# A transformer layer on one core: one gelu for each pair of row tiles, its splits and its second product in later half steps, and the coefficients of one more row tile by GpSimd

## The reference

```python
x = x + attn(layernorm(x))          # x: 8 x 1024 x 512, float32
x = x + ffn(layernorm(x))
# attn: 32 query rows of 16, causal softmax, probs in pairs:
diff = probs[:, :, 0] - lambda_full * probs[:, :, 1]     # 16 heads
attn = einsum('bhqk,bhkd->bhqd', diff, v)                # then RMS norm per head, @ Wo.T
# ffn: weights cut to -1, 0, 1
h = gelu(x @ w1_q.T + b1)           # 512 -> 2048, exact gelu
out = h @ w2_q.T + b2               # 2048 -> 512
```

## Time and profile before

| | |
|---|---|
| runs (three) | 4142.19 us median, 4137.09 to 4144.37 |
| profiled execution, its own time | 4130.02 us |
| its span, first to last instruction | 4128.2 us |
| PE, DVE, ACT, POOL busy | 81%, 80%, 70%, 43% of the span |
| mean granted TensorE clock | 0.938 of full |

### The profile page before, as it was taken

One profiled execution on the slowest core, in us unless ns is written; L12 is line 12 of the kernel. 1 busy time (PEld: TensorE's weight loads), 2 busy tenths in 40 slices (PEclk: granted clock), 3 DMA queues, 4 the chain that ended last, 5 costly groups with the idle time before them and its releaser, 6 DMA issues. The chain is left out here.

```text
span 4128.2 us, 85771 instructions
## 1 busy us (share of the span) xinstructions
PE 3339.5 (81%) x24230; PEld 2075.6 (50%) x24230; DVE 3291.2 (80%) x5317; ACT 2895.7 (70%) x6800; POOL 1780.4 (43%) x2322
## 2 busy tenths in 40 slices
PE   4787888888878888878887888878888788787888
PEld 2455555555545555545554555545455455454545
DVE  6888878888788887888778887788877888788784
ACT  4577766777667776677766777677776777667774
POOL 1255443454334543345443544435443444434444
PEclk7799999999999999999999999999999999999999
DMA  4000011100101001100011010110001010010100
GB/s 149 29 28 21 20 34 35 34 15 30 32 28 34 18 29 38 32 23 29 21 34 34 20 34 16 35 34 30 25 23 37 25 34 20 30 36 21 32 20 23
DMA packets 146896, 128.70 MB, mean 31 GB/s; under 512 B 66656, under 2 KB 117728, under 8 KB 145888
## 3 DMA queue, kind: packets, MB, share of 16 engines
q1 hardware_dynamic: 146400, 122.79, 9.1%
HBM read 67.61 MB, written 55.12 MB: 30 GB/s over the span
## 5 line engine op out<-in xcount | busy, mean ns | idle before, releaser
L632 ACT ACTIVATE E<-SP_,NM 128x256 f32<-128x256 f32 (+7 forms) x2048 | 1524.8, 745 | 968.7 <-DVE NM L801 512.9
L793 DVE TENSOR_REDUCE NM<-SP_ 128x1 f32<-128x896 f32 (+3 forms) x1024 | 1031.4, 1016 | 271.6 <-PE SP_ L1020 266.4
L1019 PE MATMUL SP_<-KST,QST 96*128 96x512 f16 (+3 forms) x3072 | 832.4, 342 | 414.6 <-ACT E L632 362.1
L820 DVE SCALAR_TENSOR_TENSOR E<-E,CC 128x512 f32<-128x512 f32 (+7 forms) x1024 | 975.1, 952 | 76.2 <-POOL CC L540 57.9
L1031 PE MATMUL DP<-ident,E 128*128 128x128 f32 x3328 | 578.6, 289 | 146.4 <-DVE E L820 135.9
L1019 PEld LDWEIGHTS SP_<-KST,QST 96*128 96x128 f16 x3072 | 272.1, 101 | 711.1 <-ACT E L632 522.1
L537 POOL TENSOR_TENSOR RP<-SUM,minus 128x1 f32<-128x1 f32 x512 | 311.7, 609 | 696.4 <-ACT E L632 686.7
L644 ACT ACTIVATE DT<-DP 128x512 f32<-128x512 f32 (+3 forms) x1024 | 526.2, 514 | 88.5 <-PE DP L1031 80.7
L1031 PEld LDWEIGHTS DP<-ident,E 128*128 128x128 f32 x3328 | 388.5, 148 | 297.0 <-issue 171.6
L801 DVE TENSOR_REDUCE NM<-SP_ 128x2 f32<-128x1024 f32 (+3 forms) x512 | 419.0, 818 | 125.0 <-PE SP_ L1020 111.3
L1076 PE MATMUL F<-X2H,W1Q 128*128 128x256 f16 x1984 | 491.5, 285 | 9.0 <-DVE SQ L930 8.4
(11 more groups left out here) (131 smaller groups left out, 5125.4 us busy)
## 6 DMA issues: line engine op xcount, KB each, us to landing
scratch<-SPL SPq DMA_DIRECT2D x65, 576.0 KB, 2.8
QST<-scratch SPq DMA_DIRECT2D x390, 64.0 KB, 2.4
X<-in_x SPq DMA_DIRECT2D x66, 256.0 KB, 2.7
out<-SQ SPq DMA_DIRECT2D x63, 256.0 KB, 2.0
KST<-scratch SPq DMA_DIRECT2D x390, 32.0 KB, 1.9
DT<-in_w1T SPq DMA_DIRECT2D x2, 1024.0 KB, 12.1
DT<-in_w2T SPq DMA_DIRECT2D x2, 1024.0 KB, 8.6
E<-in_wqT SPq DMA_DIRECT2D x1, 1024.0 KB, 8.9
```

The lines of the kernel that those rows point to most:

```text
L632: act.activation(dst, score_out(i, 2 * n + k, w), ACT.Exp, bias=NM[:, (2 * u + k) % 8:(2 * u + k) % 8 + 1], scale=1.0, accum_out=SUM[:, i ...
L793: nc.vector.tensor_reduce(NM[:, m:m + 1], score_out(i, 2 * n + k, P * (i + 1)), AX.X, ALU.max, negate=True).then_inc(max_ready, 1)
L820: nc.vector.scalar_tensor_tensor(out=E1[:, u % 4, 0:w], in0=E2[:, u % 2, 0:w], scalar=CC[:, u % 4:u % 4 + 1], in1=E1[:, u % 4, 0:w], op0=A ...
L1019: pe.matmul(SP_[:, k[a // 512], 0:n], q, KST[0:ROWS, a // P:(a + n) // P, kk, :], start=True, stop=not last)
```

## The change

The two halves of the gelu become two activations in a row at half step 0 of the even tile; `HP` now holds all 16 blocks, and `HL` is written over the first half of each row of `HP`. All eight splits stand in the even tile, at 3, 4, 5, 9, 13, 15, 17, 18. The second product of j=0 stands at 13 to 20 (two blocks each), that of j=1 at 21 to 30; its result is taken out at 20 instead of 17, and at 31 as before. Row tile 3 (four key tiles wide) gets its coefficients from GpSimd instead of DVE. In the tail ACT waits for the last second product before it writes `HP`.

```diff
+RATIO_TILE = 3
+RATIO_HEADS = N_U - H * RATIO_TILE
-GELU_ODD, GELU_EVEN = 14, 0
-SPLIT_ODD, SPLIT_EVEN = (16, 18, 20, 22), (2, 4, 6, 8)
+GELU_AT = 0
+SPLIT_AT = (3, 4, 5, 9, 13, 15, 17, 18)
-W2_LUMP, W2_REST, W2_NEXT = 1, (10, 7), (18, 13)
-OUT_AT = (17, 31)
+W2_AT = ((13, 8), (21, 10))
+OUT_AT = (20, 31)
...
-        HP = sb("HP", [P, GELU_F, 2 * P], F32)
+        HP = sb("HP", [P, FT, 2 * P], F32)
-        HL = sb("HL", [P, FT, 2 * P], F16)
+        HL = HP[:, :, :].rearrange("p a b -> p (a b)").bitcast(F16).rearrange("p (a b) -> p a b", a=FT)[:, :, 0:2 * P]
...
-                    if hs % 2 == 0 and old and old[1] >= 4:
+                    if hs % 2 == 0 and old and old[1] >= RATIO_TILE:
                         ratio(*old)
...
-            def gelu(q, j):
-                after(act, hp_ready, 8 * q + 4 * j + 4)
-                act.activation(HP[:, :, :], HP[:, :, :], ACT.Gelu).then_inc(gelu_done, 1)
+            def gelu(q):
+                after(act, hp_ready, 8 * q + 8)
+                for j in range(0, FT, GELU_F):
+                    act.activation(HP[:, j:j + GELU_F, :], HP[:, j:j + GELU_F, :], ACT.Gelu).then_inc(gelu_done, 1)
...
-            act.wait_ge(h_ready, 8 * LAST)
+            act.wait_ge(f2_ready, 2 * LAST)
...
                 if fs[0] == 0:
-                    hold(pe, h_ready, 8 * q + 4)
                     hold(pe, hp_ready, 8 * q + 8)
                     hold(pe, o_sum, 2 * q + j)
+                if j == 0:
+                    hold(pe, h_ready, 8 * q + fs[-1] // 2 + 1)
                 for f in fs:
-                    if f == GELU_F and j == 0:
-                        hold(pe, h_ready, 8 * q + 8)
```

More of the change, by code:

```diff
@@ L178, in second_product @@
             return None
-        if hs == W2_LUMP:
-            return 0, range(0, GELU_F)
-        for j, f0, (at, n) in ((0, GELU_F, W2_REST), (1, 0, W2_NEXT)):
+        for j, (at, n) in enumerate(W2_AT):
             if at <= hs < at + n:
-                return j, range(f0 + (FT - f0) * (hs - at) // n, f0 + (FT - f0) * (hs - at + 1) // n)
+                return j, range(FT * (hs - at) // n, FT * (hs - at + 1) // n)
         return None
@@ L378, in diff_attention_ffn @@
         w2f = [draw[:, 2 * FF:3 * FF], draw[:, 3 * FF:4 * FF], HH[:, :, :].rearrange("p a b -> p (a b)").bitcast(F32),
-               HL[:, :, :].rearrange("p a b -> p (a b)").bitcast(F32)]
+               HP[:, GELU_F:FT, :].rearrange("p a b -> p (a b)")]
         raw = (w1f, w2f)
         cut = [q[:, :, :].rearrange("p a b -> p (a b)") for q in (W1Q, W2Q)]
-        low = HP[:, :, :].rearrange("p a b -> p (a b)").bitcast(BF16).rearrange("p (a b) -> p a b", a=2)
+        low = HP[:, 0:GELU_F, :].rearrange("p a b -> p (a b)").bitcast(BF16).rearrange("p (a b) -> p a b", a=2)
         def hold(eng, signal, value):
@@ L403, in end_rows @@
         def end_rows(k):
-            return slice(2 * k % GELU_F, 2 * k % GELU_F + 2), slice(2 * k, 2 * k + 2)
+            return slice(2 * k, 2 * k + 2)
         block = ctx.enter_context(nc.Block())
@@ L532, in ratio @@
                 gu = b * N_U + u
-                gp = b * (N_U // 2) + u - N_U // 2
+                gp = b * RATIO_HEADS + u - H * RATIO_TILE
                 col = 8 * (n // 8) + 4 * (n % 2) + (n % 8) // 2
@@ L577, in pool_work @@
                         split(T.nb, 1)
[L578 to L581, removed]
+                    if T.w2 and hs in SPLIT_AT:
+                        hidden_split(T.pair, SPLIT_AT.index(hs))
                     if T.w2 and hs in OUT_AT:
@@ L690, in act_work @@
                         after(act, f1_ready, n + 1)
-                        after(act, h_ready, n - 3)
                         for f in (2 * k, 2 * k + 1):
-                            ins = act.activation(HP[:, f % GELU_F, :], F[:, 2 * P * (f % 2):2 * P * (f % 2) + 2 * P],
+                            ins = act.activation(HP[:, f, :], F[:, 2 * P * (f % 2):2 * P * (f % 2) + 2 * P],
                                                  ACT.Identity, bias=b1c[:, f:f + 1], scale=1.0 / XS)
                         ins.then_inc(hp_ready, 1)
[L696 to L699, removed]
+                    if T.w2 and hs == GELU_AT:
+                        gelu(T.pair)
             def abs_chunk(j, k):
@@ L705, in abs_chunk @@
                 hold(act, abs_part, 4 * j + k)
-                act.activation(HP[:, :, :].rearrange("p a b -> p (a b)"), raw[j][k], ACT.Abs,
+                act.activation(HP[:, 0:GELU_F, :].rearrange("p a b -> p (a b)"), raw[j][k], ACT.Abs,
                                accum_out=wsum[:, j, k:k + 1]).then_inc(abs_part, 1)
@@ L723, in _ @@
             every_block(act, act_work)
-            act.wait_ge(h_ready, 8 * LAST)
+            act.wait_ge(f2_ready, 2 * LAST)
             for k in range(FT // 2):
-                h, fs = end_rows(k)
+                fs = end_rows(k)
                 act.wait_ge(end_f1, k + 1)
-                if k >= 4:
-                    act.wait_ge(end_split[k % 2], (k - 4) // 2 + 1)
                 for j in range(2):
-                    ins = act.activation(HP[:, h.start + j, :], SP_[:, k % 4, 2 * P * j:2 * P * j + 2 * P], ACT.Gelu,
+                    ins = act.activation(HP[:, fs.start + j, :], SP_[:, k % 4, 2 * P * j:2 * P * j + 2 * P], ACT.Gelu,
                                          bias=b1c[:, fs.start + j:fs.start + j + 1], scale=1.0 / XS)
```

33 lines of the change are left out of this document (16 added, 17 removed).

## The result

| | before | changed |
|---|---|---|
| median of the runs, us | 4140.26 (4137.09 to 4144.37, four) | 4206.08 (4204.47 to 4208.99, four) |
| span of the profiled execution, us | 4128.2 | 4203.5 |
| mean granted TensorE clock | 0.938 | 0.918 |
| busy, us: PE, DVE, ACT, POOL | 3339.5, 3291.2, 2895.7, 1780.4 | 3327.8, 3250.8, 2817.8, 1860.1 |
| table loads | 124 | 62 |

The changed kernel is slower, at a ratio of 1.0162 (95% interval 1.0149 to 1.0175), 66 us by the medians and 75 by the profiled executions. The forecast was 4184, or +42; 4206 lies between the 4155 and 4215 that were given for the forecast itself.

The account below looks back on a forecast made before the run. No engine is full: a ring of score, row maximum, exponential, next score bounds the kernel. Terms -130 + 72 + 113 - 32 + 10 + 9 = +42 us on 4142 gave 4184, range 4092 to 4235.

Parts of the forecast that it names:

- signs of being right: Tile 5: -5 us; tile 3: -7 or more; tiles 4 and 6: +7 to 8 each; `F` wait 3+; 62 fewer loads.
- gelu leaves odd tiles: Half step 14 of odd tiles: without the gelu and its loads there, 130 us gained (bounds 111 to 151).
- coefficients of tile 3: Tile 3, coefficients moved from DVE to GpSimd: 4 us a tile, 32 us gained (bounds 0 and 56).
- gelu comes to even tiles: Half step 0 of even tiles: 1.91 us more gelu, partly covered, plus slower clock; 72 us lost (bounds 46 to 95).
- the clock's part: Start of even tiles: PE restarts at the lower clock after the gelu, costing 1.5 us in tile 6.
- second product: Half steps 13 to 30 of even tiles: extra blocks delay `F` and row maxima; 113 us lost (51 to 143).
- GpSimd, and what else is in even tiles: Tiles 4 and 6: coefficients late behind splits, 0.6 us each, 10 us lost in all (bounds 0 and 40).
- rival (d): At each table switch: it costs more than its rows show; 79 us more comes back, 4105; chance 0.02.
- Rival (a): Faster: at half step 20 `F` is complete when DVE arrives; second product costs only 51 us; 4106, chance 0.29.
- (b): No change: about half of the wait for `F` at half step 20 is covered; 4142, chance 0.11.
- Tail: Behind the last even tile: second product waits for splits and one more gelu; 9.3 us once (bounds 4, 12).
- Rival (c): GpSimd becomes the link: last split late for PE at half step 20, all even tiles; 36 us, 4221; chance 0.10.

Follow-up runs that it names:

- e3_two_gelus: Changed kernel with the first half of the gelu back at half step 14 of the odd tile: 4309.11 us, ratio 1.0418 to the kernel before.
- e8_filler: Changed kernel with 16 more multiplications on PE, result unused, at half step 1 of the even tiles: 4192.98 us, ratio 1.0125 to the kernel before.
- e1_out21: Changed kernel with the sum of j=0 taken out at half step 21 instead of 20, j=1 from 22 on: 4147.66 us, ratio 1.0038 to the kernel before.
- e7_at11: Changed kernel with j=0 of second product at half steps 11 to 18, out at 19, j=1 from 20, splits at even half steps 2 to 16: 4124.76 us.
- e2_ratio4: Changed kernel with the coefficients of row tile 3 back on DVE: 4201.7 us, ratio 1.0162 to the kernel before.
- e6_before_ratio3: Kernel before the change with only the coefficients of row tile 3 moved to GpSimd: 4146.1 us, ratio 1.0024 to the kernel before.
- e9_at11_ratio4: The kernel of e7_at11 with the coefficients of row tile 3 back on DVE: 4111.06 us, ratio 0.9939 to the kernel before.
- e4_early: Changed kernel with splits at 2 to 6 and 8 to 10, second product j=0 at 9 to 16, out at 17, j=1 from 18: 4142.66 us.
- e10_gap: The kernel of e7_at11 with the splits at 2, 4, 6, 8, 9, 10, 15, 16: 4129.26 us, ratio 0.9979 to the kernel before.
- e5_split_even: Changed kernel with its eight splits at the even half steps 2 to 16: 4201.77 us, ratio 1.0155 to the kernel before.

## Why the prediction was right or wrong

The sign, the chain of causes and the place of the largest loss were right; the sum was 33 us short of the profiled executions' difference (24 of the medians'), and one term had the wrong size altogether. Of its signs of being right, tile 5 (6.2 us shorter for 5), the wait for `F` (4.07 us for 3 or more) and the 62 loads came true; tile 3 was 4.6 us shorter where 7 or more were named, and tiles 4 and 6 were 9.7 and 6.5 us longer where 7 to 8 were. That the sum of the even tiles comes near is in part luck, as said below. Its terms, measured for one batch (four odd and four even tiles):

| term | forecast for a batch | measured |
|---|---|---|
| gelu leaves odd tiles | -16.6 | -17.2 (half steps 13 to 17) |
| odd tiles, other half steps | none | -2.8 |
| coefficients of tile 3 | -4 | 0 or a small loss |
| gelu comes to even tiles | +9.5 | +7.2 (0 and 1), and some of the clock's part later |
| second product | +14.8 | +14.1 (20 and 21) |
| GpSimd, and what else is in even tiles | +1.2 | +7.4 |

**Gelu out of the odd tiles: right, a little small.** The waits of 4.23 and 0.69 us are gone, tile 5 is 6.2 us shorter for 5.0, tile 7 5.6 for 5.3, tile 1 3.6 for 2.7. The four splits that left these tiles as well had no term of their own. `e3_two_gelus` prices the move from the other side, at about 105 us, net of what the gelu costs in the even tile.

**Tables: rival (d) is out.** By it the odd tiles would have given back 2.6 us more each, some 27 us a batch; they gave 20.0. Tiles 5 and 7 were 4.40 and 4.36 us shorter at half steps 13 to 15, where the rows had 4.47. In the rows the first gelu starts 0.02 us after the end of its load, and the load back right at the end of the second. The drain of about 1380 ns that the Trainium skill's page "ScalarE: Activation LUTs", section "What ACT_TABLE_LOAD costs", adds to each switch is not seen here: with it tiles 5 and 7 would have won some 7 us there (an estimate from that page).

**Gelu into the even tiles: right, but the clock's part lies elsewhere.** Half steps 0 and 1 grew by 1.79 us in all four tiles, the bare 1.86 us of one more gelu. I had taken 0.8 us off in tile 6 and added 1.5 for the clock at the same place. The slow clock did come, but it is paid for half steps later, where PE's delay reaches ACT: at 4 to 7. `e8_filler` shows it, at 0.9 us in tile 4; `e3_two_gelus`, where PE stands idle for one gelu instead of two, gives back the same 0.9 us there.

**Second product: right in mechanism where the V products stand in the way, and right in its sum by luck.** 3.06 us in tile 6 (forecast 5.0), 3.05 in tile 4 (4.0), 4.27 and 3.76 in tiles 0 and 2 (2.9 each, too small): 14.1 in all for 14.8, because two errors cancel. In tile 6 DVE waited 4.07 us, where I had the row maxima behind it come 4.3 us late. In tiles 0 and 2 I had counted 2.5 us of PE's work and 0.4 of waiting; measured is the wait itself, 3.5 and 2.8 us, and in tile 0 it is made longer by GpSimd: PE waits 1.35 us there in each of seven batches for the low half of a split, in front of the blocks of half step 20. Rival (a), faster because `F` is ready in time, and (b), a draw, fall with it; `e1_out21` takes most of the wait away, `e7_at11` all of it but the tail's, and they get 51 us and some 80 us back. Both move the blocks of j=1 too, and `e7_at11` the splits.

**Coefficients: the step that failed.** The prediction says "I take 4 us a tile, 8 x 4 = 32 gained; bounds 0 and 8 x 7 = 56". It measured 0 in the changed kernel (`e2_ratio4`), 10 us lost in the kernel before (`e6_before_ratio3`), and 7 to 12 lost, if all of that is the coefficients', in the best one (`e9_at11_ratio4`): at or outside the bound of 0 that I gave, for I had excluded a loss without a reason. That is 32 us of the sum, as much as the 33 that were missing; the other misses nearly cancel. Two things were not priced. GpSimd's list is in order, so that a coefficient of 0.55 + 0.21 + 0.34 us stands behind whatever split or product stands there; and the two engines' rows are longer where they run beside each other. In tile 4 of the changed kernel, GpSimd:

```profile
2325.07 2.92 POOL L565 TENSOR_TENSOR RST<-VE,nhalf 128x16 f32<-128x16 f32 x1 [1.81 <-DVE VE L900]
2327.96 0.54 POOL L536 TENSOR_TENSOR RP<-SUM,minus 128x1 f32<-128x1 f32 x1
2328.71 0.34 POOL L539 TENSOR_SCALAR CC<-RP,SUM,neglam 128x1 f32<-128x1 f32 x1 [0.21 <-POOL RP L536]
2329.01 1.26 POOL L510 TENSOR_TENSOR T<-T 128x512 f32<-128x512 f32 x1
2330.24 1.19 POOL L524 TENSOR_SCALAR HH<-HP 128x512 f16<-128x512 f32 x1
```

and DVE:

```profile
2329.08 1.87 DVE L813 SCALAR_TENSOR_TENSOR E<-E,CC 128x640 f32<-128x640 f32 x1 [1.36 <-POOL CC L539]
...
2333.75 1.65 DVE L813 SCALAR_TENSOR_TENSOR E<-E,CC 128x640 f32<-128x640 f32 x1 [1.34 <-POOL CC L539]
```

The coefficient stands behind a row of 2.92 us, and DVE waits 1.36 for it. Then DVE's combination and two rows of GpSimd run into each other: 1.87 us for the combination, which takes 0.87 at its shortest, and 1.19 for the split's first row, which took 0.62 in `e4_early` (above). The whole trace says the same: of the 128 combinations over 640 columns in the changed kernel, the 56 beside which GpSimd does nothing take 0.87 to 0.89 us each, and the other 72 take 0.87 to 1.87. The Trainium skill's page "SBUF — State Buffer", section "Who interferes with whom", says that a DVE instruction with two inputs in SBUF and a GpSimd instruction that reads SBUF shut each other out for a whole instruction; the lengthened rows agree with it, though which of GpSimd's rows held DVE up they don't tell. Its page "Perfetto Trace Analysis", section "Optimizing Scalar/DVE Operations", warns that moving work between these two engines might not help. The prediction gave the first effect one sentence ("DVE will wait for part of it") and the second none.

**GpSimd: far too small.** I took 10 us with bounds of 0 and 40. What the even tiles lost outside half steps 0, 1, 20 and 21 is 7.4 us a batch, about 59 us in all, of which tile 4 alone has 4.8. Parts of it can be told apart.

- Late coefficients. DVE's waits for them grew from 2.3 to 4.8 us in tile 4 and from 0.8 to 2.7 in tile 6, 4.4 us a batch and some 35 in all. At half steps 13 to 15 of tile 4, which took 6.54 us before and 8.34 in the changed kernel, 1.34 us of this is a wait at 15 that was not there before; in `e10_gap` it is gone and the stretch takes 6.98. The remaining 0.44 us is not explained (PE has three blocks more there). The 2.37 us in `e4_early` are the same effect.
- The clock: 0.9 us in tile 4 and 0.5 in tile 0 (`e8_filler`), and in two of eight batches 1.4 us from half step 22 of tile 6 on (windows under `e5_split_even`).

No placement that I tried removes the cost of the splits in sum, and how the rest divides was not separated: what is left at 4 to 7 of tile 4 (1.36 us at a granted clock of 1.00), and the ten blocks of PE more.

**Tail: right in kind, too small.** +12.8 us for 9, just outside its bounds of 4 and 12. The chain of the work that ended last (start, length, engine, what, line) shows the last even tile's gelu, the splits with other rows of GpSimd's list between them, and only then the second product:

```profile
4127.93 1.92 ACT HP L647
4130.76 1.15 POOL HP L526
...
4151.44 5.52 PE F L1085 x12
```

DVE's one wait of 13.3 us for `F` is this. More splits alone do not make it: in `e4_early`, with the same gelu and the same eight splits at 2 to 10, the tail is only 2.4 us longer than before. So most of it hangs on the late half steps of the splits and of the second product. Rival (c), GpSimd as the link in every even tile, does not show as a whole: PE's waits for a low half are 15.9 us in the kernel, against the 36 that it wanted. But 9.4 of them are tile 0's, 1.35 us each time; there GpSimd is the link.

**What stays open**: what makes the granted clock fall in tile 6, why tile 2, with a shorter wait for `F` than tiles 4 and 6, loses more at 20 and 21, and how the rest of the 59 us above divides.

## What to carry to other kernels

When engines run fixed lists, look for every row that reads a finished accumulation, and count what its producer does between the last useful block and the row's turn: here one half step between the two was worth 51 of the 66 us lost, and with the blocks also ahead of the products with V the change turned into a gain. Price small work that moves to a second engine by that engine's queue in front of it and by what the two share, not by the time saved on the first, and never bound it by zero on one side without a reason. Try the two halves of a compound change apart: the gelu's half was worth 105 us, and the order around it had spent them and 66 more.

## What the runs showed of the hardware

Useless work made the kernel faster. With 16 multiplications in a stall that PE had anyway (they took 5.1 us in the tile shown), the mean granted clock rose from 0.918 to 0.940, a product with V behind it took 1.93 instead of 3.64 us, and the kernel lost 10 to 15 us of its time. Against that, `e7_at11` and `e9_at11_ratio4` run at a mean clock of 0.922 and 0.921, below the 0.926 to 0.938 of the kernel before, and are faster: the mean clock alone ranks nothing. Within one stretch of fixed work it tells a lot: half steps 22 to 30 of tile 6 took 18.98 us at 0.93 and 17.63 at 1.00.

An instruction of DVE or GpSimd has no one duration here: in the changed kernel the split's first row took 0.61 to 1.57 us, its second 1.15 to 2.06, and the combination over 640 columns 0.87 to 1.87. None of the combinations that ran with GpSimd idle took more than 0.89.
